# Moving the copy of the attention output bank into the step that finishes it

## The chip, the cores and the metric

The kernel runs on 1 core of one Trainium2 chip. The metric is the device time of one execution in microseconds; the lower, the better. It computes everything in one launch, with its intermediate arrays in device memory.

## The reference

The input `x` is (16, 1024, 256): 16 batches of 1024 tokens with 256 features. One transformer layer with the norms behind the sums is computed, in fp32:

```
q, k, v = x @ Wq.T + bq, x @ Wk.T + bk, x @ Wv.T + bv      # 16 heads of 16
q, k    = rope(q) * 16 ** -0.5, rope(k)
attn    = softmax(q @ k.T)                                 # per batch and head, 1024 x 1024
x       = layernorm(x + (attn @ v) @ Wo.T + bo)
h       = relu(x @ quantize(W1).T + b1)                    # 256 -> 1024, weights in {-1, 0, 1}
out     = layernorm(x + h @ quantize(W2).T + b2)           # 1024 -> 256
```

## The kernel before

**Units, halves, steps.** The attention is worked through in units: a unit (b, g) is batch b and a group g of 4 heads (16 batches, 4 groups). A unit has two halves of 512 queries each (`qh`), and a half has 8 steps (`TT = 8`), one for each block of 128 keys. So a unit has 16 steps, numbered 0 to 15; the first half is steps 0 to 7, the second steps 8 to 15.

**What a step does.** For each of the 4 heads, TensorE makes the scores of 128 keys against 512 queries (L1030) in one of two PSUM banks `sc`, and ScalarE takes their exp into `prob` (L1193). These are called here the first, second, third and fourth score and exp of a step. A score waits until the exp two before it has freed its bank (`exp_done`), so the second score of a step waits for the fourth exp of the step before, and the fourth score for the second exp of its own step. Behind each score TensorE makes one more tile (`ms`, L1018) from which VectorE takes a maximum (L1372) for a half that comes later; there are three banks for those.

**The product with v.** The weighted sum of the values, `prob` times `v`, is made one step late: in step s TensorE runs `weigh` for step s - 1 (L1048), four matmuls of 17 rows by 512 queries, which add into one PSUM bank, `ob`. The product of a half's last step is therefore made in the first step of the next half (step 0 or 8), and only then is `ob` complete (`pv_done`). In the step after that (step 1 or 9) the product for the new half begins, and it overwrites `ob`; it waits for `o_taken`, which says that ScalarE has copied the bank to `at_st` (L1200). SyncE then stores `at_st` to device memory, from where the output projection of a later unit loads it.

**Jobs.** Into the steps TensorE also gets pieces of other work: the projections of a later batch (`e0` to `v1`) and the tail of the batch before (`t3a`, `t3b` the output projection, `t4` a transpose, `f0` to `f3` and `g0` to `g3` the two feed-forward layers). The tables `TAIL_JOBS` and `PROJ_JOBS` say in which step each of them runs: in batches 1 to 14 step 0 has `t3a`, step 1 `t3b`, step 8 `f0` and step 9 `f1`. Where a step has exactly one job and that is one of `JOBS_BEHIND` (`e0`, `o0`, `v0`, `t3a`, `f0`, `f2`, `g0`, `g2`), TensorE's order in the step is: two scores, the product with v, two scores, the job. `behind_last_pair` says whether this is so. With any other job the order is: two scores, the job, two scores, the product. Without a job the product is made in two pieces of 256 queries, one behind each pair. Batch 15 has a table of its own.

**Order of ScalarE.** ScalarE's order is written out in `batch` of the scalar block. In every step it runs the first and second exp, then what the step's jobs need of it, then the third and fourth exp. The copy of `ob` stands in step 9 ahead of the first exp, whole (512 queries), for the first half; and in step 1 for the second half of the unit before. There it is made in two pieces of 256 queries wherever steps 0 or 1 have a job: one ahead of the first exp, and one behind the second. `take_outputs` waits for `pv_done` and, before it overwrites `at_st`, for the store of the unit before. Nothing else of the order of the engines is chosen at run time: each engine runs its own list, and waits for semaphores.

Of the kernel before, what the change touches and what calls it, by code (L numbers as in the profile page):

```python
# [24 lines left out]
G = 4  # L25
# [3 lines left out]
TT = S // P  # L29
# [48 lines left out]
def projected(b, g):  # L78

    if b == 0 and g < 2:  # L80
        return [(1, 2 * g), (1, 2 * g + 1)]
    batch, quarter = (b + 1, g + 2) if g < 2 else (b + 2, g - 2)
    return [] if batch >= B else [(batch, quarter)]


def projected_next(b, g):

    return projected(b + (g + 1) // G, (g + 1) % G)[:1]
# [18 lines left out]
def last_jobs(step):  # L107

    return [("tail", last_tail(k), LAST_JOBS[r]) for k, r in last_tails_at(step) if r in LAST_JOBS]


def jobs_at(b, g, step, tail):

    if b == B - 1:
        return last_jobs(g * STEPS + step)
    found = projected(b, g)
    jobs = [("tail", (b - 1, g), TAIL_JOBS[step])] if tail and step in TAIL_JOBS else []
    return jobs + [("proj", at, table[step]) for at, table in zip(found, PROJ_JOBS.get(len(found), [])) if step in table]


def behind_last_pair(jobs):

    return len(jobs) == 1 and jobs[0][2] in JOBS_BEHIND
# [63 lines left out]
def wait_used(engine, semaphore, count):  # L187

    if count > 0:
        engine.wait_ge(semaphore, count)  # L190


def build(nc, x, xt, wqk, bqk, wv, bvc, wo, bo, w1, b1, w2, b2, rope, ident, out):
# [16 lines left out]
    with ExitStack() as ctx:  # L210
# [106 lines left out]
        late = cs_sb[:, :, :].rearrange("p i s -> p (i s)").rearrange("p (n t f) -> p n t f", t=TL, f=D)  # L317
# [29 lines left out]
        def upto(b, g, each, n):  # L347

            return b * (G * each) + (g * each + n)
# [832 lines left out]
        def _(act):  # L1182
            def finish(job_):
                stage, at, name = job_
                {"proj": proj_job, "tail": tail_job}[stage](*at, name)

            def exps(b, g, st_, j):
                n = 4 * st_ + j
                act.wait_ge(s["s2_ready"], upto(b, g, HG * STEPS, n + 1))
                if j == 0 and not (b == 0 and g == 0 and st_ < 2):  # L1190

                    act.wait_ge(s["pv_done"], upto(b, g, STEPS, st_ - 1))
                nc.scalar.activation(prob[st_ % 2][:, j, :], sc[upto(b, g, HG * STEPS, n) % SC_BANKS][:, :], ACT.Exp  # L1193
                                     ).then_inc(s["exp_done"], 1)

            def take_outputs(b, g, qh, begin=0, end=NQ):
                if begin == 0:
                    act.wait_ge(s["pv_done"], upto(b, g, STEPS, (qh + 1) * TT))
                    wait_used(act, at_stored[qh], upto(b, g, 16, 0))
                taken = nc.scalar.activation(at_st[qh][:, begin:end], ob[:, begin:end], ACT.Copy)  # L1200
                if end == NQ:
                    taken.then_inc(s["o_taken"], 1)
# [15 lines left out]
            def split_x(b, g):  # L1218

                act.wait_ge(s["xt_loaded"], upto(b, g, 16, 16) - G * 16)  # L1220
                wait_used(act, s["v_ready"], upto(b, g, 1, 0))
                nc.scalar.activation(xt_r[0][:, :, :], xt_sb[:, :, :], ACT.Copy).then_inc(s["xt_high"], 1)  # L1222
# [57 lines left out]
            def finish_rest(job_):  # L1280
                stage, at, name = job_
                if name in ("f1", "f3"):
                    take_hidden(*at, int(name[1]), job[0][:, TQ:2 * TQ])

            def batch(b, tail=True, first=False):
                for g in range(G):
                    for st_ in range(STEPS):
                        taken = []
                        if st_ == TT + 1:
                            take_outputs(b, g, 0)  # L1290
                        if st_ == 1 and not (first and g == 0):
                            taken = [(b + (g - 1) // G, (g - 1) % G, 1)]
                        in_pieces = jobs_at(b, g, 0, tail) or jobs_at(b, g, 1, tail)
                        for at in taken:
                            take_outputs(*at, 0, NQ // 2 if in_pieces else NQ)
                        exps(b, g, st_, 0)
                        exps(b, g, st_, 1)
                        if in_pieces:
                            for at in taken:
                                take_outputs(*at, NQ // 2)  # L1300
                        for job_ in jobs_at(b, g, st_, tail):
                            finish(job_)
                        if st_ == SPLIT_STEP:
                            for at in projected_next(b, g):
                                split_x(*at)
                        exps(b, g, st_, 2)
                        exps(b, g, st_, 3)
                        for job_ in jobs_at(b, g, st_, tail):
                            finish_rest(job_)
                        if st_ == SECOND_SPLIT_STEP:  # L1310
                            for at in projected(b, g)[1:]:
                                split_x(*at)
# [33 lines left out]
            split_x(1, 0)  # L1346
            act.wait_ge(s["consts_loaded"], 96)
            batch(0, tail=False, first=True)
            batch(1)
            for b in range(2, B - 2):  # L1350
                batch(b)
# [689 lines left out]
```

## Time and profile before

| | us |
|---|---|
| median of 3 runs | 3225.41 |
| lowest and highest | 3224.56, 3231.82 |
| the profiled execution, its own time | 3226.59 |
| its span, first to last instruction | 3224.8 |
| TensorE matmuls, busy | 3185.6 |
| VectorE, busy | 2972.7 |
| ScalarE, busy | 2526.4 |
| GpSimd, busy | 2154.0 |

The profiled execution's own time is 1.8 us more than its span. A busy engine is one that has an instruction in it; matmuls overlap each other and their ends are modelled, so that TensorE reads as busy while it in fact waits for a bank. Such a wait is seen in the weight loads (PEld), which stand in front of each matmul, and in the distance from one score to the next.

### The profile page before, as it was taken

How to read it: one execution, taken by the hardware profiler on the slowest of the kernel's cores; microseconds unless marked ns; L12 is line 12 of the kernel's file. 1: busy time of each engine (PE TensorE's matmuls, PEld its weight loads, DVE VectorE, ACT ScalarE, POOL GpSimd, SP SyncE). 2: the span in 40 equal slices, each digit the busy share in tenths (PEclk: the TensorE clock that was granted, in tenths of full speed). 3: DMA queues.
4: the chain of work that ended last, by engine and by line, in shares of the span. 5: the costliest groups of instructions: out<-in, count | busy, mean ns of one | idle time of the engine just before them, and what ended most of it. 6: DMA issues, size and time to landing. Idle time of an engine off the chain costs nothing.

```text
span 3224.8 us, 82324 instructions
## 1 busy us (share of the span) xinstructions
PE 3185.6 (99%) x31110; PEld 1765.9 (55%) x31110; DVE 2972.7 (92%) x5711; ACT 2526.4 (78%) x4961; POOL 2154.0 (67%) x2456
## 2 busy tenths in 40 slices
PE   6999999999999999999999999999999999999998
PEld 4445555555555555555555555555555555555556
DVE  7999999999999999999999999999999999999994
ACT  3788888888888888878878888878878888878775
POOL 2576766766766766766767767667667667665455
PEclk7999999999999999999999999999999999999999
DMA  8545354454354454453454453453553553543411
GB/s 212 118 102 119 87 115 109 97 119 113 93 119 107 98 119 104 100 120 97 105 119 101 104 119 97 109 119 90 112 118 86 117 112 93 119 104 75 99 59 41
DMA packets 312713, 342.02 MB, mean 106 GB/s; under 512 B 77373, under 2 KB 259965, under 8 KB 312317
## 3 DMA queue, kind: packets, MB, share of 16 engines
q1 hardware_dynamic: 311740, 335.97, 45.4%
q8 instruction: 246, 4.03, 0.5%
q10 hardware_dynamic: 576, 0.79, 0.2%
q14 instruction: 151, 1.23, 0.1%
HBM read 196.41 MB, written 140.24 MB: 104 GB/s over the span
## 4 chain that ended last, share of the span: by engine, by line
PE 97%; DMA 1%; DVE 1%; ACT 0%; issue 0%; POOL 0%; SPq 0%; ACTq 0%; POOLq 0%; DVEq 0%
PE ob L1048 31%; PE sc L1030 27%; PE job L787 26%; PE ms L1018 12%; PE job L838 0%; ACT prob L1193 0%; DVE mxp L1625 0%; DMA qa<-qk_parts 0%; PE sc L787 0%; SPq L482 0%; DMA os_<-wv 0%; DMA maxima<-nm 0%; POOL hid_r L1802 0%; PE ms L895 0%; DMA qk_parts<-parts 0%
## 5 line engine op out<-in xcount | busy, mean ns | idle before, releaser
L1372 DVE TENSOR_REDUCE mxp<-ms 128x1 f32<-128x512 f32 x4064 | 2604.5, 681 | 189.2 <-PE ms L1018 156.7
L1193 ACT ACTIVATE prob<-sc 128x512 f32<-128x512 f32 x4096 | 2224.0, 597 | 593.1 <-PE sc L1030 560.7
L1018 PE MATMUL ms<-ka,qa 48*128 48x512 f32 x4064 | 1494.7, 441 | 3.0 <-DVE mxp L1625 2.2
L1030 PE MATMUL sc<-qa,ka 50*128 50x512 f32 x4096 | 1495.0, 438 | 2.1 <-DMA qa<-maxima 1.1
L1030 PEld LDWEIGHTS sc<-qa,ka 50*128 50x128 f32 x4096 | 693.8, 184 | 1021.0 <-ACT prob L1193 862.0
L1048 PE MATMUL ob<-prob,v_sb 128*17 128x512 f32 (+1 forms) x8528 | 1086.5, 581 | 2.7 <-ACT at_st L1200 2.0
L1018 PEld LDWEIGHTS ms<-ka,qa 48*128 48x128 f32 x4064 | 692.4, 184 | 10.9 <-DVE mxp L1372 4.6
L1746 POOL TENSOR_TENSOR ve<-mv,eps_sb 128x2 f32<-128x2 f32 x123 | 24.1, 196 | 571.7 <-DVE mv L1399 571.7
L1767 POOL TENSOR_TENSOR hid_r<-hid,hid_r 128x512 fp32r<-128x512 f32 x248 | 319.3, 1287 | 19.9
L1048 PEld LDWEIGHTS ob<-prob,v_sb 128*17 128x17 f32 x8528 | 141.5, 95 | 312.9 <-issue 311.4
L787 PEld LDWEIGHTS job<-h_t,w_sb 64*128 64x128 f32 x3968 | 270.8, 185 | 16.1 <-issue 1.0
L787 PEld LDWEIGHTS job<-w_sb,hid_r 64*128 64x128 f32 x3968 | 269.4, 185 | 16.0 <-POOL hid_r L1767 0.7
L787 PE MATMUL job<-h_t,w_sb 64*128 64x256 f32 x3968 | 277.5, 278 | 0.0
L787 PE MATMUL job<-w_sb,hid_r 64*128 64x256 f32 x3968 | 275.8, 277 | 0.3 <-POOL hid_r L1767 0.3
L1765 POOL CAST hid_r<-hid 128x512 fp32r<-128x512 f32 x248 | 151.3, 610 | 124.1 <-DVE hid L1420 124.1
L787 PE MATMUL job<-xt_r,wqk_r 64*128 64x256 f32 x2904 | 217.3, 281 | 9.1 <-DVE wqk_r L1634 9.1
L787 PEld LDWEIGHTS job<-xt_r,wqk_r 64*128 64x128 f32 x2904 | 211.0, 188 | 23.1 <-issue 9.0
L1735 POOL TENSOR_TENSOR xt_r<-xt_sb,xt_r 128x512 fp32r<-128x512 f32 x60 | 77.5, 1292 | 141.0 <-ACT xt_r L1222 141.0
L440 POOL TENSOR_TENSOR parts<-rot,parts 128x1024 fp32r<-128x1024 f32 x60 | 143.1, 2384 | 0.2
L1247 ACT ACTIVATE hid<-job,b_sb 128x256 f32<-128x256 f32 x248 | 119.0, 480 | 17.0 <-PE job L787 5.0
L787 PE MATMUL job<-wo_sb,att_t 64*128 64x256 f32 x992 | 128.2, 375 | 0.0
L1420 DVE TENSOR_SCALAR hid<-job,b_sb 128x256 f32<-128x256 f32 x248 | 117.4, 475 | 10.7 <-PE job L787 10.7
(251 smaller groups left out, 2734.4 us busy)
## 6 DMA issues: line engine op xcount, KB each, us to landing
qk_parts<-parts SPq DMA_DIRECT2D x122, 512.0 KB, 4.3
ka<-qk_parts SPq DMA_DIRECT2D x378, 128.0 KB, 4.7
qa<-qk_parts SPq DMA_DIRECT2D x378, 128.0 KB, 7.4
attention<-at_st SPq DMA_DIRECT2D x127, 256.0 KB, 2.7
v_sb<-v_ones SPq DMA_DIRECT2D x68, 272.0 KB, 8.6
v_ones<-v_st SPq DMA_DIRECT2D x64, 272.0 KB, 2.4
xn<-x SPq DMA_DIRECT2D x63, 256.0 KB, 4.6
out<-y SPq DMA_DIRECT2D x63, 256.0 KB, 4.2
```

The lines of the kernel that those rows point to most:

```text
L440: tt(parts[:, :, :, 1, :], rot[:, :, :, :], parts[:, :, :, 0, :], ALU.subtract).then_inc(s["parts_done"], 1)
L787: done = nc.tensor.matmul(banks[out_], stationary[rows], moving[rows], start=(first and phase == 0 and n == 0), stop=(last and phase == 1 ...
L1018: nc.tensor.matmul(ms[upto(b, g, NS1, at) % MS_BANKS][:, :], operand(qa, b, unit_, j, ROWS)[:, qt * P:(qt + 1) * P], operand(ka, b, unit_, ...
L1030: nc.tensor.matmul(sc[upto(b, g, HG * STEPS, n) % SC_BANKS][:, :], operand(ka, b, unit_, j, ROWS + MROWS)[:, tt * P:(tt + 1) * P], operand ...
L1048: last = nc.tensor.matmul(ob[32 * j:32 * j + VW, begin:end], v_sb[values][:, tt, j, :], prob[st_ % 2][:, j, begin:end], start=(tt == 0 and ...
L1193: nc.scalar.activation(prob[st_ % 2][:, j, :], sc[upto(b, g, HG * STEPS, n) % SC_BANKS][:, :], ACT.Exp).then_inc(s["exp_done"], 1)
L1247: nc.scalar.activation(hid[n % 2][:, 0, :], tile, ACT.Relu, bias=b1_sb[:, 2 * n:2 * n + 1]).then_inc(s["f_even_taken"], 1)
L1372: nc.vector.reduce_max(mxp[(b * G + g) % 2][:, kh, j * TT + qt:j * TT + qt + 1], ms[upto(b, g, NS1, at) % MS_BANKS][:, :], AX.X).then_inc( ...
L1420: nc.vector.tensor_scalar(hid[n % 2][:, 1, :], tile, b1_sb[:, 2 * n + 1:2 * n + 2], 0.0, ALU.add, ALU.max).then_inc(s["f_odd_taken"], 1)
L1735: nc.gpsimd.tensor_tensor(xt_r[1][:, :, :], xt_sb[:, :, :], xt_r[0][:, :, :], ALU.subtract).then_inc(s["xt_low"], 1)
L1765: nc.gpsimd.tensor_copy(hid_r[0][:, two, :], hid[n % 2][:, :, :]).then_inc(s["hid_high"], 1)
L1767: nc.gpsimd.tensor_tensor(hid_r[1][:, two, :], hid[n % 2][:, :, :], hid_r[0][:, two, :], ALU.subtract).then_inc(s["hid_low"], 1)
```

## The change

Where the first step of a half (0 or 8) has its product with v behind the second score, ScalarE copies the whole bank `ob` in that same step, behind the second exp and ahead of the third. Elsewhere the copy stays in step 1 or 9 as it was. Only ScalarE's list is changed.

```diff
@@ batch of the scalar block @@
                         taken = []
-                        if st_ == TT + 1:
+                        early = st_ % TT == 0 and behind_last_pair(jobs_at(b, g, st_, tail))
+                        late = st_ % TT == 1 and not behind_last_pair(jobs_at(b, g, st_ - 1, tail))
+                        if late and st_ == TT + 1:
                             take_outputs(b, g, 0)
-                        if st_ == 1 and not (first and g == 0):
+                        if late and st_ == 1 and not (first and g == 0):
                             taken = [(b + (g - 1) // G, (g - 1) % G, 1)]
                         in_pieces = jobs_at(b, g, 0, tail) or jobs_at(b, g, 1, tail)
                         for at in taken:
                             take_outputs(*at, 0, NQ // 2 if in_pieces else NQ)
                         exps(b, g, st_, 0)
                         exps(b, g, st_, 1)
+                        if early and st_ == TT:
+                            take_outputs(b, g, 0)
+                        elif early and not (first and g == 0):
+                            take_outputs(b + (g - 1) // G, (g - 1) % G, 1)
                         if in_pieces:
                             for at in taken:
                                 take_outputs(*at, NQ // 2)
```

Of the 128 copies of the kernel, the last stands behind all steps and is not touched. Of the 127 others, 119 move by the tables: 57 in steps 0 with `t3a` (all 56 of batches 1 to 14 and one of batch 15), one in a step 0 with `g2` (batch 15), 57 in steps 8 with `f0`, one in a step 8 with `g0` (batch 15), and 3 in batch 0 with `e0`. 8 stay, 4 in batch 0 and 4 in batch 15.

The first place is ScalarE's list around steps 0 and 1 of batch 5, group 0. Before, with four exps of step 0 (`prob0`), then step 1 (`prob1`) with the two pieces:

```order
L1193 ACTIVATE prob0<-sc0 128x512 [waits pv_done,s2_ready]
L1193 ACTIVATE prob0<-sc1 128x512 [waits s2_ready]
L1193 ACTIVATE prob0<-sc0 128x512 [waits s2_ready]
L1193 ACTIVATE prob0<-sc1 128x512 [waits s2_ready]
L1200 ACTIVATE at_st1<-ob 128x256 [waits at_stored1,pv_done]
L1193 ACTIVATE prob1<-sc0 128x512 [waits pv_done,s2_ready]
L1193 ACTIVATE prob1<-sc1 128x512 [waits s2_ready]
L1200 ACTIVATE at_st1<-ob 128x256
L1193 ACTIVATE prob1<-sc0 128x512 [waits s2_ready]
L1193 ACTIVATE prob1<-sc1 128x512 [waits s2_ready]
```

The same place of ScalarE's list now:

```order
L1193 ACTIVATE prob0<-sc0 128x512 [waits pv_done,s2_ready]
L1193 ACTIVATE prob0<-sc1 128x512 [waits s2_ready]
L1200 ACTIVATE at_st1<-ob 128x512 [waits at_stored1,pv_done]
L1193 ACTIVATE prob0<-sc0 128x512 [waits s2_ready]
L1193 ACTIVATE prob0<-sc1 128x512 [waits s2_ready]
L1193 ACTIVATE prob1<-sc0 128x512 [waits pv_done,s2_ready]
```

The two pieces have gone from step 1, and one whole copy stands between the second and third exp of step 0.

The second place is ScalarE's list around steps 8 and 9 of batch 4, group 3, whose copy was whole already. Before:

```order
L1193 ACTIVATE prob0<-sc0 128x512 [waits pv_done,s2_ready]
L1193 ACTIVATE prob0<-sc1 128x512 [waits s2_ready]
L1193 ACTIVATE prob0<-sc0 128x512 [waits s2_ready]
L1193 ACTIVATE prob0<-sc1 128x512 [waits s2_ready]
L1200 ACTIVATE at_st0<-ob 128x512 [waits at_stored0,pv_done]
L1193 ACTIVATE prob1<-sc0 128x512 [waits pv_done,s2_ready]
L1193 ACTIVATE prob1<-sc1 128x512 [waits s2_ready]
L1247 ACTIVATE hid0<-job0,b1_sb 128x256 [waits hid_low,f_ready]
```

And now:

```order
L1193 ACTIVATE prob0<-sc0 128x512 [waits pv_done,s2_ready]
L1193 ACTIVATE prob0<-sc1 128x512 [waits s2_ready]
L1200 ACTIVATE at_st0<-ob 128x512 [waits at_stored0,pv_done]
L1193 ACTIVATE prob0<-sc0 128x512 [waits s2_ready]
L1193 ACTIVATE prob0<-sc1 128x512 [waits s2_ready]
L1193 ACTIVATE prob1<-sc0 128x512 [waits pv_done,s2_ready]
L1193 ACTIVATE prob1<-sc1 128x512 [waits s2_ready]
L1247 ACTIVATE hid0<-job0,b1_sb 128x256 [waits hid_low,f_ready]
```

The copy has moved past two exps; behind it stand the third and fourth exp of step 8. The lists of TensorE, VectorE, GpSimd and SyncE have the same instructions in the same order in both kernels.

## Rows read from the trace of the kernel before

**Rows 1.** The page: busy time of the engines, share of the span, instructions.
```profile
PE 3185.6 (99%) x31110; PEld 1765.9 (55%) x31110; DVE 2972.7 (92%) x5711; ACT 2526.4 (78%) x4961; POOL 2154.0 (67%) x2456
```
**Rows 2.** The page: costliest groups; behind the bar busy us, mean ns, idle before.
```profile
L1030 PEld LDWEIGHTS sc<-qa,ka 50*128 50x128 f32 x4096 | 693.8, 184 | 1021.0 <-ACT prob L1193 862.0
L1018 PEld LDWEIGHTS ms<-ka,qa 48*128 48x128 f32 x4064 | 692.4, 184 | 10.9 <-DVE mxp L1372 4.6
```
**Rows 3.** The instructions that write `at_st`: durations (ns), forms; TensorE's waits.
```profile
L1200 ACT ACTIVATE at_st<-ob x189: 383/393/617, 102.9 to 3186.4; 128x256 f32<-128x256 f32 x122, 128x512 f32<-128x512 f32 x67
...
  PE ob L1048: 2.0, 3
```
**Rows 4.** ScalarE's timeline, steps 0 and 1 of batch 5, group 0: start, us, instruction.
```profile
1040.46 1.08 ACT L1193 ACTIVATE prob<-sc 128x512 f32<-128x512 f32 x2 [0.56 <-PE sc L1030]
1042.10 1.09 ACT L1193 ACTIVATE prob<-sc 128x512 f32<-128x512 f32 x2 [0.56 <-PE sc L1030]
1043.07 0.39 ACT L1200 ACTIVATE at_st<-ob 128x256 f32<-128x256 f32 x1
1043.44 1.08 ACT L1193 ACTIVATE prob<-sc 128x512 f32<-128x512 f32 x2
1044.41 0.39 ACT L1200 ACTIVATE at_st<-ob 128x256 f32<-128x256 f32 x1
```
**Rows 5.** TensorE's timeline, the same two steps.
```profile
1040.59 1.05 PE L1048 MATMUL ob<-prob,v_sb 128*17 128x512 f32 x8
...
1042.82 0.92 PE L1030 MATMUL sc<-qa,ka 50*128 50x512 f32 x2
1043.24 0.18 PEld L1030 LDWEIGHTS sc<-qa,ka 50*128 50x128 f32 x1 [0.26 <-ACT prob L1193]
...
1044.26 0.58 PE L1030 MATMUL sc<-qa,ka 50*128 50x512 f32 x1
...
1044.57 0.18 PEld L1030 LDWEIGHTS sc<-qa,ka 50*128 50x128 f32 x1 [0.15 <-ACT prob L1193]
1044.68 0.39 PE L1030 MATMUL sc<-qa,ka 50*128 50x512 f32 x1
```
**Rows 6.** ScalarE's timeline, the last unit (batch 15, group 3), steps 8 and 9.
```profile
3163.48 0.60 ACT L1200 ACTIVATE at_st<-ob 128x512 f32<-128x512 f32 x1 [0.25 <-PE ob L1048]
3163.97 1.08 ACT L1193 ACTIVATE prob<-sc 128x512 f32<-128x512 f32 x2
```
**Rows 7.** TensorE's timeline, the last unit: the product before that copy.
```profile
3162.36 1.05 PE L1048 MATMUL ob<-prob,v_sb 128*17 128x512 f32 x8
```
**Rows 8.** ScalarE's timeline, steps 8 and 9 of batch 4, group 3.
```profile
1017.47 1.09 ACT L1193 ACTIVATE prob<-sc 128x512 f32<-128x512 f32 x2 [0.56 <-PE sc L1030]
1018.44 0.60 ACT L1200 ACTIVATE at_st<-ob 128x512 f32<-128x512 f32 x1
1018.91 1.11 ACT L1193 ACTIVATE prob<-sc 128x512 f32<-128x512 f32 x2
```
**Rows 9.** TensorE's timeline, the same two steps.
```profile
1015.96 1.05 PE L1048 MATMUL ob<-prob,v_sb 128*17 128x512 f32 x8
...
1018.61 0.18 PEld L1030 LDWEIGHTS sc<-qa,ka 50*128 50x128 f32 x1
...
1019.90 0.39 PE L1030 MATMUL sc<-qa,ka 50*128 50x512 f32 x1
...
1020.12 0.44 PE L1030 MATMUL sc<-qa,ka 50*128 50x512 f32 x1
```
**Rows 10.** Stretches, steps 1 and 9: length; busy PE, PEld, DVE, ACT, POOL; clock; DMA.
```profile
1042.82:1045.99 3.17, 3.17 (x28) 1.54 (x25) 3.17 (x8) 3.07 (x7) 0.00 (x0) 1.00 1.05 131
1018.45:1021.49 3.04, 3.04 (x36) 1.71 (x32) 2.91 (x6) 2.97 (x8) 2.16 (x4) 1.00 0.23 86
```
**Rows 11.** TensorE's timeline, third and fourth score of step 11 (batch 4, group 3).
```profile
1026.10 0.39 PE L1030 MATMUL sc<-qa,ka 50*128 50x512 f32 x1
...
1026.33 0.39 PE L1030 MATMUL sc<-qa,ka 50*128 50x512 f32 x1
```

## The prediction

> **What bounds the kernel now.** I read the busy times first. They are to show which engine is full: TensorE has a matmul in it for 3185.6 of 3224.8 us, VectorE is at 92%, ScalarE at 78% [rows 1]. So time on ScalarE costs something only where TensorE waits for it. The costliest groups say where that can be: the weight loads of the scores stand idle for 862.0 us until an exp ends, those of the maximum tiles only 4.6 us until VectorE ends [rows 2]. Most of the 862 us lies beside a product or a job that is still running in the array, and costs nothing. Which part is real can be read only from the timeline of the steps that the change touches: steps 0 and 1 [rows 4, 5] and steps 8 and 9 [rows 8, 9]. The reader is to look there for the second and the fourth score of the step behind the moved copy, since those wait for an exp.
>
> In step 1 the second score's weight load starts at 1043.24, 0.05 behind the end of the fourth exp of step 0 (1042.10 + 1.09 = 1043.19), and the two scores together take 0.92 us [rows 4, 5]. The third and fourth score of the same step, behind the same kind of job, take 1044.26 to 1045.07, 0.81 us, and the fourth ends 0.23 behind the third (1044.84), which is the distance of an unheld pair (1026.10 to 1026.33) [rows 5, 11]. So TensorE is held by about 0.11 us at the second score of step 1, by the fourth exp of step 0, and not measurably at the fourth. In step 9 the second score's weight load starts at 1018.61, again 0.05 behind the end of the fourth exp of step 8 (18.56) [rows 8, 9]: the exp sets it there too, with nothing to spare. And the fourth score of step 9 ends at 1020.56, 0.27 behind the third (1020.29), where 0.23 is normal; its exp, the second of step 9, ended at 1020.02 [rows 8, 9, 11]. That is a loss of about 0.045 us.
>
> **What the change takes away.** The copy leaves steps 1 and 9. In step 9 it ran from 1018.44, and the exps behind it took 1.11 us as a pair instead of 1.09 [rows 8]. Without it the pair starts as soon as its first score is done and takes 1.09, and the fourth score is no longer held: the 0.045 us are given back. Bounds: nothing, and 0.06 us with the rounding of the rows, since an unheld score can't come closer than 0.23. In step 1 the pieces lie at 1043.07 and 1044.41 [rows 4]. The exps behind the first piece may come forward, but the score that waits for them, the fourth, is not held now; the second piece stands behind the second exp and in front of nothing that TensorE waits for. I take 0 there; the upper bound is the 0.15 us of idle weight load at the fourth score [rows 5], which by the 0.23 above is not real.
>
> ScalarE itself saves time: a piece makes the next exp start 0.37 later, two of them 0.74, the whole copy 0.49 [rows 4, 6]. 59 pairs become whole, some 15 us of ScalarE. None of it is on the path, since the engine idles between the pairs of exps (0.56 us in front of each in step 0) [rows 4]. The Trainium skill (Perfetto Trace Analysis, Optimizing Scalar/DVE Operations) puts the fixed cost of a ScalarE instruction on PSUM at about 51 ns and says that grouping helps where the engine is saturated; by that figure the 59 mergers would be an estimated 3.0 us, all of it in the sum if ScalarE set the pace and none if it doesn't. The trace has the second case.
>
> **What it adds.** The copy now stands between the second and third exp of steps 0 and 8. It can't start before the product is complete. In step 0 the product ends at 1040.59 + 1.05 = 1041.64, in step 8 at 1017.01 [rows 5, 9]. The trace has one whole copy that waited for its product: the product ended at 3162.36 + 1.05 = 3163.41, the copy started at 3163.48, 0.07 later, and the exp behind it at 3163.97, 0.49 after the copy's start [rows 6, 7]. So the third exp starts at 1041.64 + 0.07 + 0.49 = 1042.20 instead of 1042.10, and in step 8 at 1017.57 instead of 1017.47 [rows 4, 8]: 0.10 us late in both. The gap between the pairs of exps is long enough for a copy (0.56), but the product ends in the middle of it. The fourth exp follows back to back, and is 0.10 late as well.
>
> Behind the waiting copy on ScalarE stand only those two exps; nobody waits for the third in time (the first score of the next step, at 1042.82, comes behind the job in the array, and a third exp from 1042.20, about 0.60 long, ends at 1042.80) [rows 5, 6]. For the fourth exp waits the second score of the next step, and it has no slack in either kind of step. So it starts 0.10 us later, and what is queued behind it on TensorE in order (the job, the other two scores, the product) follows 0.10 later. Bounds of this term: 0.08, if the chain through the exps gives back their start-up overlap, and 0.12 with the rounding of the rows. I take 0.10.
>
> What else moves: the wait for `o_taken` in front of the next product ends earlier by more than a microsecond, but TensorE waited for the copy only 3 times and 2.0 us in the whole kernel, so that is 0 [rows 3]. The store of `at_st` goes out earlier in step 8; in step 0 SyncE has other transfers in front of it. Nobody waits for the store inside the unit: 0, bound ±1 us for the whole. The waits on VectorE: it is full in step 1, 3.17 of 3.17 us [rows 10], but later tiles only give it slack.
>
> **The sum.** 57 copies go into a step 0 with `t3a`: 57 x 0.10 = 5.7 us. 57 into a step 8 with `f0` and one into a step 8 with `g0`, whose next steps have the pattern of step 9: 58 x (0.10 - 0.045) = 3.2 us. One goes into a step 0 with `g2`: 0.1. The three of batch 0 have short `e0` jobs, where both scores are held by exps; there loss and return are both larger, and I set them to -0.3 together. That is 8.7 us; with the third figure of the terms open, and the first of them more likely below 0.10 than above (the exp pair behind the waiting copy takes 1.08, one hundredth less than 1.09) [rows 4, 6], I take 8.3 us. The profiled execution would go from 3226.59 to 3234.9. It lies 1.2 us above the median of the runs shown, 3225.41; from there the forecast is 3233.7, which is 0.26% slower.
>
> **The rivals.**
> - *The next step gives nothing back, or the hold is longer.* The 0.10 falls due in full in each of the 116 places in batches 1 to 15, and as a late second score also makes its exp late, the fourth score may be held too. For it: rows 9 show that this score is the one with no reserve in step 9. Against: the exp of the second score may start only 0.49 behind the first anyway. Price: 116 x 0.10 = 11.6 us, up to 116 x 0.12 = 13.9; time 3237.0.
> - *The delay is swallowed.* VectorE is busy for 3.17 of 3.17 us in step 1 and 2.91 of 3.04 in step 9 [rows 10]. If it sets TensorE's pace there through its three banks, a late score only fills a wait that would come anyway. Against: 4.6 us of waiting for it in all [rows 2]. Price: 0, or with 58 x 0.045 returned -2.6; time 3222.8 to 3225.4, so 3224.5.
> - *Faster.* The copy is the reason for the holds in step 1, and with it they go. The Trainium skill (Perfetto Trace Analysis, Optimization Strategy) says to find the gap on the most contended engine and to make what ends it start sooner; by that rule, taking the copy out of steps 1 and 9 is right, since the holds there are ended by exps. For it: the idle 0.26 and 0.15 stand in the step where the copies stood [rows 5]. Against: the exp that ends the 0.26 is the fourth of step 0, which ran ahead of the copy. Price: 57 x 0.11 + 58 x 0.045 = 8.9 us; time 3216.5. It decides if the third exp isn't later than 1042.10, so if the copy costs the exps less than 0.39 us.
> - *It doesn't do what it says.* 119 of 127 copies move in ScalarE's list, so this could only be that the copy waits so long that it delays nothing new; that is in the second rival.
>
> **How the numbers follow.** About 0.3% (9.7 us) is what a measurement of this kernel can tell from no change; from 3225.4 that is 3215.7 and 3235.1. Forecast 0.66, its own range 3230.5 to 3236 (8 x the bounds 0.08 and 0.12 of 116 places, with the run-to-run difference of 1 us); about a seventh of it lies above 3235.1. First rival 0.18, all slower. Second 0.12, all the same. Third 0.04, which I count as faster, since its price is at the line. So faster 0.04, same 0.57 + 0.12 = 0.69, slower 0.09 + 0.18 = 0.27. The range 3226 to 3238 leaves out the third rival, most of the second and the top of the first.
>
> **What would show it.** Right: the third exp of steps 0 and 8 0.56 us behind the product's end instead of 0.46; the second score of step 1 ending 0.10 farther from the first (the two take 1.02 instead of 0.92), that of step 9 too; the fourth score of step 9 again 0.23 behind the third; step 1 at 3.27 instead of 3.17, step 9 at 3.09 instead of 3.04, steps 0 and 8 as long as before; 59 fewer instructions of ScalarE. Wrong: a third exp that is not late (then the third rival), steps 2 or 10 shorter by what steps 1 and 9 lose (the second), or a fourth score in step 1 or 9 that is held longer than now (the first).

## The result and the profile after

| | before | after |
|---|---|---|
| median, us | 3225.37 | 3232.70 |
| lowest and highest of the runs | 3223.16, 3231.82 | 3231.10, 3234.45 |
| runs | 12 | 12 |
| ratio, 95% interval | | 1.0023 [1.0015, 1.0030] |
| span of the profiled execution | 3224.8 | 3232.0 |
| ScalarE, busy | 2526.4 | 2531.3 |
| instructions of ScalarE | 4961 | 4902 |

The changed kernel is 7.3 us slower; 3233.7 was forecast, 8.3 us more. Medians here and below leave out three slow executions, two of the kernel before and one of the doubled copy, which took 1.5 to 1.8 times as long as the others. The page's busy times, which answer to [rows 1], show the same engine full for the same share:

```profile
PE 3192.6 (99%) x31110; PEld 1767.2 (55%) x31110; DVE 2980.0 (92%) x5711; ACT 2531.3 (78%) x4902; POOL 2154.1 (67%) x2456
```

TensorE is busy 7.0 us longer with the same 31110 matmuls. The instructions that write `at_st` [rows 3] are now these; the second line is the idle time of ScalarE in front of them that ended with the product, in us and times, where the kernel before has 1.2 and 3:

```profile
L1200 ACT ACTIVATE at_st<-ob x130: 384/598/617, 101.9 to 3193.6; 128x512 f32<-128x512 f32 x126, 128x256 f32<-128x256 f32 x4
...
  PE ob L1048: 21.2, 122
```

59 pairs of pieces have become whole copies, as ScalarE's list says, and each of the 119 moved copies waits for its product. ScalarE's timeline of steps 0 and 1 of batch 5, group 0 after the change, to be held against [rows 4]:

```profile
1042.66 1.09 ACT L1193 ACTIVATE prob<-sc 128x512 f32<-128x512 f32 x2 [0.56 <-PE sc L1030]
1043.91 0.60 ACT L1200 ACTIVATE at_st<-ob 128x512 f32<-128x512 f32 x1 [0.16 <-PE ob L1048]
1044.40 1.08 ACT L1193 ACTIVATE prob<-sc 128x512 f32<-128x512 f32 x2
1045.64 1.08 ACT L1193 ACTIVATE prob<-sc 128x512 f32<-128x512 f32 x2 [0.15 <-PE sc L1030]
```

The copy waits 0.16 us for the product, starts, and the third exp stands 0.49 behind it. TensorE's timeline of the same two steps, with the weight load of the second score, answers to [rows 5]:

```profile
1042.79 1.05 PE L1048 MATMUL ob<-prob,v_sb 128*17 128x512 f32 x8
...
1045.05 0.55 PE L1030 MATMUL sc<-qa,ka 50*128 50x512 f32 x1
...
1045.54 0.49 PE L1030 MATMUL sc<-qa,ka 50*128 50x512 f32 x1
...
1045.54 0.18 PEld L1030 LDWEIGHTS sc<-qa,ka 50*128 50x128 f32 x1 [0.30 <-ACT prob L1193]
```

The product ends at 1043.84, the copy starts 0.07 later and the third exp 0.56 behind the product's end, where it was 0.46 before. This holds in all places: over the 112 steps 0 and 8 of batches 1 to 14 the third exp stands 0.561 us behind the product's end instead of 0.462, and none differs from these means by more than 0.004. The second score of step 1 ends at 1046.03, 0.98 behind the start of the first, where it was 0.92; its weight load waits 0.30 instead of 0.26 for the fourth exp of step 0, and the first score itself starts 1.21 behind the product's end, where it was 1.18. Steps 8 and 9 of batch 4, group 3, first ScalarE, then TensorE, answer to [rows 8, 9]:

```profile
1018.00 1.09 ACT L1193 ACTIVATE prob<-sc 128x512 f32<-128x512 f32 x2 [0.63 <-PE sc L1030]
1019.25 0.60 ACT L1200 ACTIVATE at_st<-ob 128x512 f32<-128x512 f32 x1 [0.16 <-PE ob L1048]
1019.74 1.08 ACT L1193 ACTIVATE prob<-sc 128x512 f32<-128x512 f32 x2
```

```profile
1018.13 1.05 PE L1048 MATMUL ob<-prob,v_sb 128*17 128x512 f32 x8
...
1020.63 0.74 PE L1030 MATMUL sc<-qa,ka 50*128 50x512 f32 x2
...
1022.17 0.62 PE L1030 MATMUL sc<-qa,ka 50*128 50x512 f32 x2
```

In the kernel before, the second score of step 9 was this one:

```profile
1018.69 0.41 PE L1030 MATMUL sc<-qa,ka 50*128 50x512 f32 x1
```

The first two scores of step 9 take 0.74 us, where they took 1018.45 to 1019.10 = 0.65 (the first one's start is the stretch's in [rows 10]); the last two 0.62, which is one matmul of 0.39 and the normal distance of 0.23, where they took 0.66. So in this example 0.09 is lost at the second score and 0.04 given back at the fourth; averaged over batches 1 to 13 it is 0.097 and 0.057. The stretches of the four steps (length, then busy PE, PEld, DVE, ACT, POOL), steps 0, 1, 8 and 9:

```profile
1042.13:1045.05 2.92, 2.92 (x29) 1.50 (x25) 2.90 (x7) 2.23 (x5) 0.00 (x0) 1.00 0.75 178
1045.05:1048.29 3.24, 3.24 (x30) 1.59 (x26) 3.24 (x7) 2.61 (x5) 0.00 (x0) 1.00 1.07 142
1017.46:1020.63 3.17, 3.17 (x37) 1.86 (x34) 2.54 (x5) 2.47 (x5) 3.17 (x3) 1.00 0.00 0
1020.63:1023.71 3.08, 3.08 (x38) 1.67 (x34) 2.96 (x6) 2.62 (x7) 2.06 (x4) 1.00 0.26 90
```

Step 1 takes 3.24 instead of 3.17 and step 9 3.08 instead of 3.04 [rows 10]. Averaged over batches 1 to 13, from the first score of a step to that of the next, step 0 goes from 2.896 to 2.924, step 1 from 3.169 to 3.232, step 8 stays at 3.165 and step 9 goes from 3.036 to 3.076; no other step differs by more than 0.01. That is 0.13 us a unit and 7.4 us for the 56 units of batches 1 to 14. Step 2 gives back 0.5 us in all (2.941 to 2.935), so that these batches take 6.8 us more. The rest of the 7.2 us between the spans is +0.5 in batch 15, -1.4 in batch 0, and 1.3 by which the steps begin later. Nothing can be read from the last two: the kernel without a moved copy (the instruction without its wait, below) also has a batch 0 that is 1.2 shorter, and begins 1.5 earlier.

### The profile page after: what moved, and what is told of

Its sections match the earlier page's. It is cut to its first block, busy times and chain, and to the rows that moved or that the text cites. A ratio compares the mean times of both kernels' runs of the same rounds, so it can differ in the third digit from the quotient of the medians.

```text
span 3232.0 us, 82265 instructions
## 1 busy us (share of the span) xinstructions
PE 3192.6 (99%) x31110; PEld 1767.2 (55%) x31110; DVE 2980.0 (92%) x5711; ACT 2531.3 (78%) x4902; POOL 2154.1 (67%) x2456
## 4 chain that ended last, share of the span: by engine, by line
PE 97%; DMA 1%; DVE 1%; ACT 0%; issue 0%; POOL 0%; SPq 0%; ACTq 0%; POOLq 0%; DVEq 0%
PE ob L1048 31%; PE sc L1030 28%; PE job L787 26%; PE ms L1018 11%; PE job L838 0%; ACT prob L1193 0%; DVE mxp L1631 0%; PE sc L787 0%; DMA qa<-qk_parts 0%; DMA maxima<-nm 0%; SPq L482 0%; PE ms L895 0%; DMA os_<-wv 0%; POOL hid_r L1808 0%; DMA qk_parts<-parts 0%
## 5 line engine op out<-in xcount | busy, mean ns | idle before, releaser
L1426 DVE TENSOR_SCALAR hid<-job,b_sb 128x256 f32<-128x256 f32 x248 | 118.0, 477 | 10.7 <-PE job L787 10.7
```

The costliest lines, as they stand in the source:

```text
L1426: nc.vector.tensor_scalar(hid[n % 2][:, 1, :], tile, b1_sb[:, 2 * n + 1:2 * n + 2], 0.0, ALU.add, ALU.max).then_inc(s["f_odd_taken"], 1)
```

## The experiments

All times are medians. The kernel before was measured beside each set: 3224.8 beside the two kernels with one place alone, the whole copy in the old place and the pieces of 256; 3225.5 beside the copy without a wait, the doubled, the shorter and the later one; 3226.0 beside the pieces of 384 and the changed kernel again. With the 9 to 11 executions that most kernels have here, an interval is about 0.1% (3 us) to each side.

**One place alone.** The first two kernels move the copy in one of the two kinds of step only.

```diff
-early = st_ % TT == 0 and behind_last_pair(jobs_at(b, g, st_, tail))
-late = st_ % TT == 1 and not behind_last_pair(jobs_at(b, g, st_ - 1, tail))
+early = st_ == TT and behind_last_pair(jobs_at(b, g, st_, tail))
+late = st_ == 1 or (st_ == TT + 1 and not behind_last_pair(jobs_at(b, g, st_ - 1, tail)))
```

This is the first; the second has `st_ == 0` in `early`, and in `late` the two kinds of step exchanged.

> Of the two places only steps 8 move their copy (59 copies: 57 with f0, g0, two with e0... in batch 0); steps 0 and 1 are as in the kernel before. My theory (the copy waits for the product, makes the third and fourth exp 0.10 us late, and the second score of the next step falls due late; step 9 gets 0.045 to 0.055 us back): step 9 grows from 3.04 to 3.08 us, step 1 stays at 3.17; 58 x 0.045 = 2.6 us more than before, about 3228.0. Rival (nothing is given back in step 9, the return seen comes from elsewhere): 58 x 0.10 = 5.8 us, 3231.2. Rival (the whole loss belongs to the merging of pieces in step 1): 3225.4.

Measured 3227.69, ratio 1.0010 [1.0001, 1.0019]: 2.9 us, where 58 x 0.045 = 2.6 was expected. It moves 60 copies and not 59: in its trace 60 more copies wait for their product than before. Its steps 1 and 9:

```profile
1040.65:1043.82 3.17, 3.17 (x28) 1.53 (x25) 3.17 (x8) 3.06 (x7) 0.00 (x0) 1.00 1.08 140
...
1016.22:1019.30 3.08, 3.08 (x36) 1.66 (x33) 2.96 (x6) 2.62 (x7) 2.12 (x4) 1.00 0.26 90
```

> Only steps 0 move their copy (and make one whole copy out of two pieces); steps 8 and 9 are as before. My theory: step 1 grows from 3.17 by 0.06 and step 0 by 0.03 us, together 0.09 us for each of 58 units, 5.2 us; 3230.6. It adds up with the kernel that moves only steps 8 to the whole change. Rival (the loss belongs to step 9): 3225.4. Rival (the two places disturb each other): the two losses don't add up to the 7.3 us of the whole change within 1.5 us.

Measured 3230.59, ratio 1.0017 [1.0009, 1.0026]: 5.8 us. Its steps 0, 1 and 9:

```profile
1041.22:1044.14 2.92, 2.92 (x30) 1.48 (x26) 2.90 (x7) 2.23 (x5) 0.00 (x0) 1.00 0.75 182
1044.14:1047.38 3.24, 3.24 (x30) 1.56 (x26) 3.24 (x7) 2.60 (x5) 0.00 (x0) 1.00 1.04 139
...
1019.75:1022.78 3.03, 3.03 (x36) 1.70 (x32) 2.91 (x6) 2.96 (x8) 2.05 (x4) 1.00 0.23 87
```

Each kernel has the loss in its own pair of steps and nothing in the other, and the two losses, 8.6 us together, are the whole change (7.3 in its first set of runs, 8.3 in the second, below) within what the runs can tell. The two places don't disturb each other, and none of the rivals named for these two kernels stands.

**The instruction without its wait.** To the kernel before, one more copy is added in the place where the change puts its own; it reads a constant tile and waits for nothing.

```diff
                         exps(b, g, st_, 1)
+                        if st_ % TT == 0 and behind_last_pair(jobs_at(b, g, st_, tail)) and not (b == g == st_ == 0):
+                            nc.scalar.activation(spare[:, :], wo_sb[:, :, :].rearrange("p c f -> p (c f)"), ACT.Copy)
```

> The kernel before with one more ScalarE instruction in the place of the moved copies (behind the second exp of the same 119 steps): a copy of 512 elements of a constant SBUF tile into a tile that nobody reads, which waits for nothing. It separates the instruction from its wait. My theory: it starts right behind the second exp, ends its turn before the third score is ready (the pairs of exps are 0.56 apart), and costs nothing: third exp still 0.46 behind the product's end, 3224.9. Rival (any instruction of 0.5 us in this place makes the exps late, with or without the wait): 119 x 0.05 to 0.10, 3231 to 3237.

Measured 3226.03, ratio 1.0000 [0.9991, 1.0009]. ScalarE in step 0 of batch 5, group 0:

```profile
1037.79 1.08 ACT L1194 ACTIVATE prob<-sc 128x512 f32<-128x512 f32 x2 [0.56 <-PE sc L1031]
1038.76 0.63 ACT L1300 ACTIVATE spare<-wo_sb 128x512 f32<-128x512 f32 x1
1039.43 1.09 ACT L1194 ACTIVATE prob<-sc 128x512 f32<-128x512 f32 x2
```

and TensorE's product beside it:

```profile
1037.92 1.05 PE L1049 MATMUL ob<-prob,v_sb 128*17 128x512 f32 x8
```

The added copy is longer than the moved one (0.63 against 0.60), starts 0.28 earlier against the product's end (0.21 ahead of it instead of 0.07 behind), and the third exp is 0.46 behind the product's end as in the kernel before. 119 of these instructions cost nothing that the runs can tell. So it is not an instruction between the exps that costs, but its start. (This one reads SBUF and not PSUM; that a copy from PSUM in the same place, with the same wait, is free too if it is short enough, is shown by the shorter copy below.)

**Twice the work in the place.**

```diff
                         if early and st_ == TT:
+                            copy_again(b, g, 0)
                             take_outputs(b, g, 0)
```

(and the same in steps 0; `copy_again` waits for `pv_done` and copies `ob` into a tile `spare` that nobody reads.)

> The changed kernel with the moved copy made twice: a second one of the same size, into a tile that nobody reads, in front of each of the 119 moved copies. My theory: a copy in that place has no cover left, so its 0.49 us go through in full: third and fourth exp 0.59 late instead of 0.10, second score of the next step too; 119 x 0.49 = 58 us more than the changed kernel (3232.7), about 3291. Rival (the 0.10 is a fixed price of a wait for TensorE's product and the place has slack for ScalarE's work): 3233 to 3240.

Measured 3290.27 (three executions), ratio 1.0201 [1.0183, 1.0220]: 57.6 us above the changed kernel, where 119 x 0.49 = 58.3 was expected. ScalarE in step 0, where the product ended at 1058.02 + 1.05 = 1059.07:

```profile
1059.14 0.60 ACT L1207 ACTIVATE spare<-ob 128x512 f32<-128x512 f32 x1 [0.16 <-PE ob L1049]
1059.63 0.59 ACT L1201 ACTIVATE at_st<-ob 128x512 f32<-128x512 f32 x1
1060.11 2.28 ACT L1194 ACTIVATE prob<-sc 128x512 f32<-128x512 f32 x4
```

The third exp is 1.04 behind the product's end. Averaged over batches 1 to 13, steps 0 and 1 together take 0.49 us more than in the changed kernel, and steps 8 and 9 together 0.49 too. Behind the waiting copy there is no cover left; ScalarE's time there is the kernel's time.

**A shorter copy.**

```diff
-                            take_outputs(b, g, 0)
+                            take_outputs(b, g, 0, 0, 384)
```

(and the same in steps 0.) The kernel leaves out the other 128 columns; two memsets, about 1 us together, fill `at_st` at the start.

> The changed kernel, whose moved copies take only 384 of the 512 queries; the other 128 columns of at_st are not copied, and keep what was there. (At the start two memsets on GpSimd fill at_st, some us at most.) My theory: a copy of 384 makes the next exp start about 0.39 later instead of 0.49, which is all that the gap has behind the product: third exp at 0.46 to 0.47 behind the product's end, step 1 back to 3.17 to 3.18, step 9 at 2.99: 3222 to 3223, with up to 1 us for the start. Rival (the price does not depend on the length): 3232.7. Rival (the copy must be far shorter, since the wait for the product costs more than 0.07): 3226 to 3230.

Measured 3222.52, ratio 0.9991 [0.9982, 1.0000]. ScalarE in step 0, then TensorE's product (ended at 1038.79) and third score:

```profile
1038.86 0.49 ACT L1200 ACTIVATE at_st<-ob 128x384 f32<-128x384 f32 x1 [0.17 <-PE ob L1048]
1039.25 1.09 ACT L1193 ACTIVATE prob<-sc 128x512 f32<-128x512 f32 x2
```

```profile
1037.74 1.05 PE L1048 MATMUL ob<-prob,v_sb 128*17 128x512 f32 x8
1038.72 0.49 PE L1030 MATMUL sc<-qa,ka 50*128 50x512 f32 x1
```

The copy waits just as long and starts the same 0.07 behind the product, but the next exp comes 0.39 behind it, on time at 0.46. So the price depends on the length, and is gone at 384 columns. The 0.39 is the gap and not the time that the copy takes: the exp starts 0.04 behind the end of its score (1038.72 + 0.49 = 1039.21), as in each of the 119 places, and would not start earlier without the copy. How long ScalarE is taken by a shorter copy shows only where the exp behind it doesn't wait for its score, as in step 1 of batch 0, group 3 of the kernel before:

```profile
126.51 0.39 ACT L1200 ACTIVATE at_st<-ob 128x256 f32<-128x256 f32 x1
126.78 0.62 ACT L1193 ACTIVATE prob<-sc 128x512 f32<-128x512 f32 x1
```

There it is 0.26 for 256 columns, and 0.26 again in the only other such place of that trace; for 512 columns it is 0.48, and 0.49 behind a wait. By these two, 384 columns would take an estimated 0.37.

**Whole in the old place.** The kernel before, with step 1's copy whole ahead of the first exp, separates the merging of the pieces from their move.

```diff
-                            take_outputs(*at, 0, NQ // 2 if in_pieces else NQ)
+                            take_outputs(*at)
```

(and without the second piece.)

> The kernel before with the copy in step 1 whole in front of the first exp, instead of in two pieces; step 9 as before (whole). It splits the merging from the moving. My theory: the first exp of step 1 starts 0.49 behind the start of the copy instead of 0.37, so 0.12 late, and with it the second, for which the fourth score waits without any reserve (it is 0.23 behind the third now): the fourth score comes about 0.11 late, step 1 takes 3.28, 59 x 0.11 = 6.5 us more, about 3231.9. Rival (merging only saves time of ScalarE, and the loss of the change is all of the moving): 3225.4, step 1 at 3.17. Rival (fewer instructions help): below 3225.

Measured 3231.11, ratio 1.0020 [1.0012, 1.0029]: 6.3 us, where 59 x 0.11 = 6.5 was expected. In the trace step 1 takes 0.136 more on average, 7.6 us in batches 1 to 14, of which step 2 gives back 0.7. The weight loads of the second and the fourth score of step 1:

```profile
1043.63 0.18 PEld L1030 LDWEIGHTS sc<-qa,ka 50*128 50x128 f32 x1 [0.26 <-ACT prob L1193]
...
1045.10 0.18 PEld L1030 LDWEIGHTS sc<-qa,ka 50*128 50x128 f32 x1 [0.28 <-ACT prob L1193]
```

The second waits 0.26 as before, but the fourth 0.28 instead of 0.15 [rows 5]. With pieces it has next to no reserve, and a whole copy in front of its exp holds it by the 0.13 that it adds. The saved instructions earn nothing.

**Pieces in the new place.** If only what stands behind the waiting copy counts, a piece that takes ScalarE at most 0.39 there is free, and the rest can go behind the fourth exp, beside the job.

```diff
-                        if early and st_ == TT:
-                            take_outputs(b, g, 0)
-                        elif early and not (first and g == 0):
-                            take_outputs(b + (g - 1) // G, (g - 1) % G, 1)
+                        moved = []
+                        if early and st_ == TT:
+                            moved = [(b, g, 0)]
+                        elif early and not (first and g == 0):
+                            moved = [(b + (g - 1) // G, (g - 1) % G, 1)]
+                        for at in moved:
+                            take_outputs(*at, 0, NQ // 2)
...
                         exps(b, g, st_, 3)
+                        for at in moved:
+                            take_outputs(*at, NQ // 2)
```

> As the changed kernel, but in steps 0 and 8 the copy is made in two pieces of 256 queries: one behind the second exp, one behind the fourth. A piece makes the next exp start about 0.28 to 0.37 us later, the gap behind the product has 0.39. My theory: the third exp is on time again (0.46 behind the product's end), step 1 is 3.17 us as before, step 9 is 2.99 instead of 3.04 since the whole copy no longer stands in front of its exps; 58 x 0.05 = 2.9 us less than before, about 3222.6. Rival (an instruction behind the product costs the exps a fixed time, whatever its length): the same loss as the changed kernel or more, 3232.7. Rival (step 9 gives nothing back of itself): 3225.4.

Measured 3221.48, ratio 0.9991 [0.9982, 1.0000]. ScalarE in step 8 of batch 4, group 3 and the start of step 9, then the stretches of steps 1 and 9:

```profile
1013.64 0.38 ACT L1200 ACTIVATE at_st<-ob 128x256 f32<-128x256 f32 x1 [0.17 <-PE ob L1048]
1014.04 1.08 ACT L1193 ACTIVATE prob<-sc 128x512 f32<-128x512 f32 x2
1015.01 0.39 ACT L1200 ACTIVATE at_st<-ob 128x256 f32<-128x256 f32 x1
1015.44 1.09 ACT L1193 ACTIVATE prob<-sc 128x512 f32<-128x512 f32 x2
```

```profile
1039.32:1042.50 3.18, 3.18 (x28) 1.55 (x25) 3.18 (x8) 2.80 (x6) 0.00 (x0) 1.00 1.04 137
...
1015.02:1018.00 2.98, 2.98 (x37) 1.70 (x33) 2.86 (x6) 2.81 (x8) 2.13 (x4) 1.00 0.23 88
```

Step 1 is as before the change, step 9 is 0.06 shorter. The same with the split at 384 queries, beside the changed kernel:

```diff
-                            take_outputs(*at, 0, NQ // 2)
+                            take_outputs(*at, 0, 3 * NQ // 4)
```

> The kernel with two pieces, split at 384 instead of 256 queries: 384 behind the second exp, the last 128 behind the fourth of steps 0 and 8. It asks how long a piece may be. My theory: the next exp starts 0.39 behind a piece of 384, and the gap has 0.39 from the earliest start of the copy to the third score: on the edge, third exp at most 0.02 late; the same time as with the split at 256 within 1.5 us, 3221.5 to 3223. Rival (the piece must leave room, the edge is lower): 3225 or more.

> The changed kernel once more, beside the kernel with pieces of 384 and 128 queries on one chip, so that the two can be compared directly: 3232.7, 10 us above it by my theory (0.09 and 0.10 us for each of 58 units and halves); under 5 us if what the pieces win is a matter of the chip or of the day.

Measured 3222.15, ratio 0.9989 [0.9980, 0.9998], and 3234.24, ratio 1.0026 [1.0016, 1.0036]. The two kernels differ by 12.1 us; they differ in nothing but the cut through the copy and the place of its smaller part. Against the kernel before, the version with pieces is 3.4 and 3.8 us ahead in the two sets of runs. That is about 0.1%, with one interval just below 1 and one that touches it: too little to be called shown by time alone. In the steps of the traces it is plain: step 9 takes 2.981 on average with either split instead of 3.036, 3.0 us in batches 1 to 14.

**Later instead of earlier.** The last one looks at the other end of the window: the whole copy of step 9 behind the second exp of step 9.

```diff
-                        if st_ == TT + 1:
-                            take_outputs(b, g, 0)
...
                         exps(b, g, st_, 1)
+                        if st_ == TT + 1:
+                            take_outputs(b, g, 0)
```

> The kernel before with the whole copy of step 9 behind the second exp of step 9 instead of ahead of the first; step 1 as before. My theory of what waits for the copy at the other end: the copy then starts near 0.98 behind the first exp and ends some 0.6 later, about 0.03 us before the product of step 9 wants to start; the product needs some 0.14 from the copy's end to its start, so it is held by about 0.1, while the fourth score is no longer held (0.05): step 9 is 3.05 to 3.15, 3225 to 3231. Rival (the product has slack, as it waits for the copy only 3 times in the kernel before): the 0.05 us are won and nothing lost, 3222.

Measured 3248.37 (four executions), ratio 1.0072 [1.0058, 1.0085]: 23 us, far above both expectations; the execution in the trace is the slowest of the four, and its span is 24.6 us longer than before. The first part is as I had it: step 9 takes 3.13 instead of 3.04, since the product starts late, which is 5.3 us in batches 1 to 14.

```profile
1030.60:1033.73 3.13, 3.05 (x36) 1.73 (x33) 3.01 (x7) 2.81 (x7) 2.10 (x4) 1.00 0.08 29
```

I had overlooked the steps 9 in which no job stands between the second score and the product: two without a job in batch 0, and two in batch 15, by its own table. There TensorE now waits 1.5 us for the copy. Its timeline in batch 0, group 2:

```profile
196.62 0.63 PE L1048 MATMUL ob<-prob,v_sb 128*17 128x256 f32 x8 [1.52 <-ACT at_st L1200]
```

The stretches of that step and of the next ones (the column behind POOL is the granted clock), then the stretch behind the same wait in group 3, and the one behind the same wait in batch 15, group 0:

```profile
194.37:198.40 4.03, 2.51 (x29) 0.97 (x26) 2.36 (x5) 2.45 (x6) 3.85 (x3) 1.00 0.17 65
198.40:203.50 5.10, 5.10 (x32) 1.81 (x28) 3.21 (x6) 2.59 (x5) 4.92 (x5) 0.51 0.01 3
203.50:208.40 4.90, 4.90 (x30) 1.47 (x32) 3.08 (x5) 2.78 (x6) 2.75 (x2) 0.50 0.00 0
208.40:212.00 3.60, 3.60 (x36) 1.28 (x28) 3.48 (x8) 2.65 (x5) 2.38 (x4) 0.95 0.03 5
...
246.30:259.90 13.60, 13.34 (x80) 4.12 (x80) 7.44 (x14) 6.39 (x13) 6.53 (x6) 0.50 0.19 61
...
3036.75:3046.75 10.00, 10.00 (x98) 6.08 (x98) 7.94 (x15) 7.17 (x14) 6.17 (x6) 1.00 0.85 187
```

Behind the 1.5 us of idle TensorE in batch 0 the granted clock is 0.50, the lower level of 1.2 GHz, for 10.2 us the first time and 13.7 us the second. Batch 0 alone takes 10.7 us more than in the kernel before, with these two places. The same wait is not always followed by the lower clock. Behind the one in batch 15, group 0, the clock stays at 1.00; behind the one in group 3 it is 0.50 for 3.4 us; and the kernel before has a wait of nearly this length, in step 1 of batch 15, group 2, with the clock at 1.00 behind it:

```profile
3090.58 0.62 PE L1048 MATMUL ob<-prob,v_sb 128*17 128x512 f32 x4 [1.42 <-ACT at_st L1200]
```

What makes the difference stays open. Batch 15 takes 4.1 us more in all. A third price is in step 11 of group 3 in batches 1, 5, 9 and 13: the store of `at_st` goes out later (in batch 5 it is issued 5.2 us behind the start of step 8 instead of 3.8), the denominators land late, and VectorE waits for them, 0.5, 1.9, 1.6 and 0.3 us. In batches 5 and 9 TensorE then waits for VectorE. VectorE and TensorE in step 11 of batch 5, group 3:

```profile
1234.89 0.35 DVE L1427 RECIPROCAL rden<-den 128x32 f32<-128x32 f32 x1 [1.89 <-DMA den<-attention]
```

```profile
1235.84 0.50 PE L1018 MATMUL ms<-ka,qa 48*128 48x512 f32 x1 [1.12 <-DVE mxp L1372]
```

Step 11 takes 3.3 us more in batches 1 to 14; step 10 takes 1.8 us more, for which I have no cause.

## Why the prediction was right, point by point

- *What bounds the kernel, and which scores wait for an exp.* Right. The price lies in the second score behind the moved copy (and, by 0.03 us, in the first score of step 1); the doubled copy passes its 0.49 us through, in both kinds of step.
- *The copy can't start before 0.07 behind the product, and the exp follows 0.49 later.* Right to the hundredth: third exp 0.56 behind the product's end in all 112 places of batches 1 to 14. That the wait is needed for the loss is shown by the copy without a wait, and that it is wait plus length by the copy of 384 queries. The forecast took both numbers from a single instruction of the kernel before [rows 6, 7]; that they hold for all others was not known then.
- *0.10 us in steps 0 and 1.* Measured 0.028 + 0.063 = 0.091. I had put all of it into step 1 (3.27); a part appears in step 0, since the first score of step 1 starts 0.03 late, which I had set to 0. The reserve of 0.02 that I read for it (a third exp that ends at 1042.80, a score that starts at 1042.82) wasn't one: its weight load stood at 1042.79, and in the changed kernel it starts at 1045.05, 0.05 behind the end of the third exp (1044.40 + 0.60), by which it is now held. The two take 0.98 and not the 1.02 of my sign. The sum is 0.01 less: 0.5 us for 57 places.
- *0.10 less 0.045 in step 9.* Measured 0.040 net: 0.097 lost and 0.057 given back on average. So what comes back was read too small from the one example (0.045), and 0.7 of the 0.9 us that this term lacks is there; the kernels with pieces give back the same 0.055.
- *Nothing for the merging.* Right for the place it has after the change. In the old place it costs 6.3 us, because of the fourth score, of which I said only that it was not measurably held; it had next to no reserve, and the prediction did not need that. What I said of ScalarE's own saving was misread: the exp 0.37 behind the first piece [rows 4] started 0.04 behind the end of its score, which the trace has at 1043.40, so 0.37 is again a gap. A piece takes 0.26 where nothing else holds the exp, two of them 0.53, the whole copy 0.48. 59 pairs are thus some 3 us of ScalarE and not 15, which is the size that the 3.0 us set beside it had. None of it was in the sum.
- *Batch 0 at -0.3, the waits of TensorE for the copy at 0, the store at 0.* TensorE waits for the copy 1.8 us in all instead of 2.0. The other two are not contradicted, but not shown either: batch 0 differs by more than a microsecond between executions whatever the copy does.
- *The sum.* With the measured sizes it is 57 x 0.091 + 58 x 0.040 + 0.1 - 0.3 = 7.3 instead of 8.7. The 0.4 us that I took off by judgment went the right way, without a term behind it. The range of 3230.5 to 3236 doesn't follow from its words: the bounds 0.08 and 0.12 in 116 places, less 58 x 0.045, give 6.7 to 11.3 us more, 3232.1 to 3236.7. The measured 3232.70 lies in both. That the total came out as near as 0.03% is in part luck, since 1 us is also what the first and the second set of runs of the same change differ by (7.3 and 8.3).
- *The rivals.* The first fails by the fourth score of step 9, which is back at 0.23; the second by the doubled copy and by the step lengths, since steps 2 give back 0.5 of the 7.4 us and steps 10 nothing; the third because with the copy out of step 1 the weight load of the second score still waits for the fourth exp of step 0, and longer (0.30). The Trainium skill's rule that went with it (Perfetto Trace Analysis, Optimization Strategy: make what ends the gap start sooner) isn't contradicted by these traces: what ended the gap was an exp, and the change made that exp 0.10 us later.

## What to carry to other kernels

Between two waits an engine has a window, and the window for an instruction begins when what it waits for is there, not when the engine falls idle: here ScalarE was idle for 0.56 us, but only 0.39 of it lay behind the earliest start of the copy. How much of the window an instruction takes is read where nothing else holds the one behind it; where that one starts on time, one reads the window instead. What does not fit is paid by whoever waits for the instructions queued behind; here nearly in full, 0.091 of 0.10 us, and in full when the copy was doubled. The cure that worked here is to cut the instruction at the window's size and put the rest beside the next long job. Before a copy is moved later instead, look at each step in which no job stands ahead of the product, for there the other end of the window is much nearer.

## What the runs showed of the hardware

- Behind a wait of 1.5 us of TensorE the granted clock stood at 0.50 for 10.2, 13.7 and 3.4 us in three places of the kernel with the later copy, and stayed at 1.00 in a fourth; behind 1.42 us in the kernel before it stayed at 1.00 too. In batch 0 the two waits themselves were 3.0 of the 10.7 us lost.
- A ScalarE copy from PSUM into SBUF takes less of the engine than its own length says. The next exp starts 0.48 us behind the start of a copy of 512 fp32 columns (0.49 if the copy waited for its product), and 0.26 behind one of 256, while their own lengths are given as 0.60 and 0.39. The difference between start and next start is the number to fit into a gap, and it is to be read where the next instruction waits for nothing else.
- A copy that waits for a finished product starts 0.07 us behind its end, in each of the 112 places of batches 1 to 14.
